# Gated cross-attention and MoE block: the beginning of the kernel rebuilt, keys made batch by batch

## The chip, the cores and the metric

One core of one Trainium2 chip. The figure is device time in microseconds (us) of one execution; it is measured over three runs and the median is compared. TensorE (PE), VectorE (DVE), ScalarE (ACT), GpSimd (POOL) and SyncE (SP, which here only issues DMAs) each run their own instructions in program order and wait for each other by semaphores.

## What is computed

Four batches of 256 positions of width 256 pass through gated cross-attention to a context of width 64 (16 query heads, 4 key heads, head width 16), and then through a second gated block: causal attention with 16 heads of width 128, and a mixture of four experts.

```python
x = x + tanh(g_xattn[0]) * xattn(layernorm(x), ctx, ctx, q_norm_w, k_norm_w, w_out)
x = x + tanh(g_ffn[0]) * ffn(layernorm(x), ...)      # attention 16x128, then MoE, top 2 of 4

def xattn(q, k, v, q_norm_w, k_norm_w, w_out):
    q, k = rms_norm(q, q_norm_w), rms_norm(k, k_norm_w)
    q, k = q * cos + rotate_half(q) * sin, k * cos + rotate_half(k) * sin   # per head of 16
    scores = einsum('bgnqd,bgkd->bgnqk', q, k) / sqrt(16)                   # causal mask, softmax
    return (softmax(scores) @ v).reshape(B, T, 256) @ w_out.T
```

## The kernel before

Everything stays in SBUF; a position is a partition, so a batch b is two tiles t of 128 positions. The change touches only what leads into cross-attention and the first part of it.

**The packed operands.** Scores are made by bf16 products that keep float32 accuracy: a query or key head of 16 numbers is split in three bf16 parts (value, rest, rest of the rest), and the parts are repeated in eight *slots* of 16, which fill the 128 rows of a product. Queries of a batch are made in two halves X of 8 heads. `qpack` (written as q_room) and `kpack` (written as V) hold these slots, and PE turns them (eight transpositions each: `q_turn(b, X, t)` L1161, `k_turn(b)` L1150) into PSUM banks 6 and 7, from where ACT (`q_evac` L527) copies them to qT (qk_room) and DVE (`k_out` L802) to kT (yacc). Each of the two banks serves a fixed order of users (the lists M6 and M7), and each user waits until the one ahead has been copied out.

**The beginning.** DVE takes the statistics of batch 0 (`stats(0, 2)`, L743 and L746), then, once ACT has summed the squares of all eight context tiles (L517), runs three Newton steps for ten reciprocal roots (L723 to L725), normalizes the queries of batch 0 (`norm_q(0)`, L763), and makes the keys of all four batches at once (L768 to L787) with the tables WKC and WKS that POOL makes first (L329 to L331). POOL goes on with the query tables WC and WS (L338 to L340) and `prep(b, X)` (L353 to L366), which rotates one half of the queries and writes three of the eight slots. `pack(b, X)` on DVE (L793 to L797) fills the other five.

**The pieces.** Scores then go in 48 pieces p, twelve to a batch (k is the piece in its batch b). In a piece PE runs `x_scores(p)` (L1204, L1205), DVE takes the maxima (`x_max(p)`, L894), PE makes the scores again transposed and shifted by the maxima (`x_turned(p - 3)`, L1218 to L1230), ACT exponentiates them (`x_exp`, L563), and every third piece PE multiplies by the values (`x_values`, L1245) and turns the result (`o_turn`, L1255). `x_scores(p)` waits for the maxima of piece p - 2. Each engine has its own hand-written sequence over p; between the pieces stand the preparations of the next batch: on DVE `norm_q(b + 1)` at k = 1, `pack(b + 1, 0)` at k = 6, `pack(b + 1, 1)` at k = 11, and from batch 1 on the residual and the norm of the batch before; on PE `q_turn(b, 1, t)` at k = 3 and 4, `q_turn(b + 1, 0, t)` at k = 9 and 10, and `out_turn` and `out_project` at k = 8 and 9.

In POOL's order after prep(0, 1) come the copies of the context into the value slots (L392), and then prep(1, 0), prep(1, 1), prep(2, 0) and so on; the split of the first weights of the next stage follows prep(3, 1) (L403 and on).

## Time and profile before

| | us |
|---|---|
| median of 3 runs | 477.19 (476.87 to 477.73) |
| the profiled execution, its own time | 475.73 |
| its span, first to last instruction | 473.9 |
| first maxima of a piece (p = 0) start | 30.12 |
| first maxima of batch 1 (p = 12) start | 47.41 |
| last maxima (p = 47) start | 113.0 |

Busy shares over the whole span: PE 87%, DVE 81%, POOL 60%, ACT 58%. The profile's rows give the start of an instruction or a group from the span's start, its duration, engine, line and tiles; the bracket behind gives the idle time of that engine just before and what ended it. The rows used are shown further down.

### The profile page before, as it was taken

To read this page: it belongs to the slowest core of one execution; us is meant where nothing else is said; L and a number is where in the kernel's file an instruction comes from. 1 tells how busy PE (TensorE), PEld (TensorE's weight loads), DVE (VectorE), ACT (ScalarE), POOL (GpSimd) and SP (SyncE) were. 2 spreads that over 40 slices of the span, in tenths; PEclk is the share of its full clock that TensorE was granted. 3 is DMA by queue.
4 is the path that set the end of the run, shared out by engine and by line. 5 is a ranking of instruction groups with operands and counts; after the bars stand their busy time and mean duration, and the time that the engine had idled before them with its cause. 6 is when DMAs were issued, how large, how long until landed. Compare 5 with 4: busy or idle time off the path is not lost.

```text
span 473.9 us, 10279 instructions
## 1 busy us (share of the span) xinstructions
PE 413.9 (87%) x3150; PEld 360.1 (76%) x3150; DVE 383.0 (81%) x1185; ACT 273.6 (58%) x617; POOL 286.0 (60%) x385
## 2 busy tenths in 40 slices
PE   0179998889899699999999999999999996678994
PEld 0157876667677599899899899898998995567894
DVE  4886769695889688798797897898898768867997
ACT  2036655554235567766767687677677688175440
POOL 5956718902299557777587586687687544153541
PEclk9999999999999799999999999999999998799998
DMA  8200000200245496585775765775865754000011
GB/s 279 57 3 1 2 1 3 89 2 1 46 100 123 85 190 134 127 201 109 160 169 117 181 145 109 190 138 117 194 134 111 145 89 92 20 0 2 0 46 44
DMA packets 71347, 44.53 MB, mean 94 GB/s; under 512 B 57360, under 2 KB 59536, under 8 KB 71312
## 3 DMA queue, kind: packets, MB, share of 16 engines
q1 hardware_dynamic: 67392, 35.42, 35.2%
q10 hardware_dynamic: 3920, 8.69, 6.6%
q8 instruction: 17, 0.28, 0.2%
q14 instruction: 18, 0.15, 0.1%
HBM read 13.68 MB, written 1.05 MB: 31 GB/s over the span
## 4 chain that ended last, share of the span: by engine, by line
PE 64%; DVE 21%; POOL 6%; issue 5%; ACT 2%; DMA 2%; ACTq 0%; SPq 0%; DVEq 0%; POOLq 0%
PE bank L1264 35%; PE bank L1332 5%; PE bank L1378 5%; DVE yacc L1119 3%; PE bank L1331 3%; PE bank L1379 3%; DVE yacc L1128 2%; DVE nxm L894 2%; PE bank L1245 2%; PE bank L1204 2%; PE bank L1182 2%; DMA rows_sb<-in_rows 1%; POOL room L435 1%; PE bank L1161 1%; PE bank L1205 1%
## 5 line engine op out<-in xcount | busy, mean ns | idle before, releaser
L630 ACT ACTIVATE probs<-sm,nm 128x128 f32<-128x128 f32 (+1 forms) x128 | 56.9, 447 | 43.3 <-DVE nm L1005 43.3
L622 ACT ACTIVATE probs<-turned 128x768 uint16<-128x768 uint16 x64 | 69.1, 1079 | 20.9 <-DMA turned<-halves 20.0
L1264 PE MATMUL bank<-hH,qk_parts 128*128 128x512 f32 x240 | 75.6, 396 | 0.0
L447 POOL COPY halves<-probs 128x768 uint16<-128x768 uint16 x64 | 52.8, 825 | 37.3 <-DVE probs L1051 36.5
L435 POOL TENSOR_TENSOR room<-room,qk_room 128x512 f32<-128x512 f32 x32 | 41.3, 1293 | 34.6 <-DMA qk_room<-qk_room 29.5
L1264 PE MATMUL bank<-hL,qk_parts 128*128 128x512 f32 x120 | 58.3, 486 | 0.5 <-DVE room L922 0.4
L1264 PEld LDWEIGHTS bank<-hH,qk_parts 128*128 128x128 f32 x240 | 45.5, 190 | 9.6
L922 DVE SCALAR_TENSOR_TENSOR room<-bank,qk_bias,cst_sb 128x512 f32<-128x512 f32 x64 | 47.4, 740 | 0.0
L1264 PE MATMUL bank<-woH,o_parts 128*128 128x256 f32 x256 | 47.3, 283 | 0.0
L1264 PE MATMUL bank<-woL,o_parts 128*128 128x256 f32 x128 | 38.8, 303 | 6.5 <-DVE yacc L1042 2.5
L435 POOL TENSOR_TENSOR room<-room,q_room 128x512 f32<-128x512 f32 x32 | 41.2, 1290 | 5.4 <-DMA q_room<-q_room 5.4
L1264 PE MATMUL bank<-wvL,hH 128*128 128x256 f32 x128 | 39.3, 307 | 5.0 <-POOL wvL L380 4.3
L639 ACT ACTIVATE o_parts<-bank,bv_pair 128x256 fp32r<-128x256 f32 x64 | 30.0, 468 | 19.1 <-PE bank L1379 12.7
L563 ACT ACTIVATE probs<-bank 128x512 f32<-128x512 f32 x48 | 28.5, 596 | 21.5 <-PE bank L1230 12.6
L894 DVE TENSOR_REDUCE nxm<-bank 128x2 bf16<-128x512 f32 (+1 forms) x48 | 32.4, 686 | 10.0 <-PE bank L1205 9.6
L1264 PEld LDWEIGHTS bank<-woH,o_parts 128*128 128x128 f32 x256 | 39.6, 190 | 0.0
L1378 PE MATMUL bank<-probs,V 128*128 128x256 f32 x128 | 39.3, 390 | 0.0
L1332 PE MATMUL bank<-room 128*128 128x256 f32 x128 | 38.7, 384 | 0.0
L1264 PE MATMUL bank<-wvH,hH 128*128 128x256 f32 x128 | 36.6, 286 | 0.0
L1264 PE MATMUL bank<-wvH,hL 128*128 128x256 f32 x128 | 36.6, 286 | 0.0
L527 ACT ACTIVATE qk_room<-bank 128x1024 bf16<-128x1024 bf16 x16 | 16.4, 1024 | 34.8 <-PE bank L1161 34.8
L922 DVE SCALAR_TENSOR_TENSOR qk_room<-bank,qk_bias,cst_sb 128x512 f32<-128x512 f32 x32 | 24.0, 749 | 15.3 <-PE bank L1264 15.1
(216 smaller groups left out, 1268.8 us busy)
## 6 DMA issues: line engine op xcount, KB each, us to landing
qk_room<-qk_room SPq DMA_DIRECT2D x64, 128.0 KB, 2.4
q_room<-q_room SPq DMA_DIRECT2D x64, 128.0 KB, 2.4
stg<-in_wqkv ACTq DMA_DIRECT2D x6, 768.0 KB, 5.4
stge<-in_we ACTq DMA_DIRECT2D x7, 256.0 KB, 3.0
stg<-in_wqkv SPq DMA_DIRECT2D x2, 768.0 KB, 6.2
stgo<-in_wo ACTq DMA_DIRECT2D x6, 256.0 KB, 3.3
x_sb<-in_x SPq DMA_DIRECT2D x4, 256.0 KB, 6.1
turned<-halves SPq DMA_TRANSPOSE x64, 2.8
```

The source lines that it names most:

```text
L435: pool.tensor_tensor(v, v, qk_sw[q], ALU.subtract).then_inc(s["rope_done"], 1)
L447: pool.tensor_copy(halves[:, j % 2, :, :], PR[:, j % 2, 0:384].bitcast(U16).rearrange("p (n h) -> p h n", h=2)).then_inc(s["b_split"], 1)
L527: act.activation(qT[:, X, t, :, :].rearrange("p h n -> p (h n)"), bank_bf[0][:, :], ACT.Copy).then_inc(s["m6_free"], 1)
L563: act.activation(prob_slot(m, z), PT_B[p % 2][:, :], ACT.Exp).then_inc(s["s_exp"], 1)
L622: act.activation(PTs[:, 1 - q, 0:384].bitcast(U16).rearrange("p (n h) -> p h n", h=2), turned[:, (j - 3) % 4, :, :].rearrange("p (h c) n - ...
L630: ins = act.activation(PR[:, q, a:e], sm[:, q, a:e], ACT.Exp, bias=nm[:, q, t:t + 1], scale=-1.0, accum_out=rs[:, q, t:t + 1])
L639: act.activation(oH[:, ((j - 4) // 2) % 2, q, :], value_bank(j)[:, 0:256], ACT.Identity, bias=head_bias(j)).then_inc(s["b_oH"], 1)
L894: dve.tensor_reduce(nxm[:, m % 3, a:a + len(heads)], S_B[p % 2][:, :].rearrange("p (h n) -> p h n", h=len(heads)), AX.X, ALU.max, negate=T ...
L922: return dve.scalar_tensor_tensor(out.rearrange("p (b t) -> p b t", b=2), source[:, :].rearrange("p (b t) -> p b t", b=2), qk_bias[:, c:c ...
L1264: ins = pe.matmul(outp, l, r, start=(m == 0), stop=(m == n - 1))
L1332: pe.matmul(S_B[j % 2][:, P:3 * P], QT[:, 2 * r, second], QT[:, 2 * r + 1, both], start=True, stop=True).then_inc(s["b_s"], 1)
L1378: pe.matmul(value_bank(j)[:, 0:256], V[:, 2 * b, r * HD:(r + 1) * HD], PTs[:, q, 0:256], start=True, stop=False)
```

## The change

- **Loads.** SP issues x of batch 0, then only the strict mask and the small rope tables, then the identity on a semaphore of its own, and then waits for x of batch 0 and the first rows before it issues the rest. ACT issues the first 320 columns of the rows and the context of batch 0; the other three batches of the context and the rest of the rows it issues after two sums of squares.
- **ACT** makes the bf16 identity and mask (DVE did), sums squares one at a time (each waits for the one ahead, since all write one scratch tile), waits for both late loads ahead of the third, and fills the slots of batch 0's queries and keys (`q_slots`, `k_slots`).
- **DVE** waits for two sums of squares and not eight, and roots four numbers and not ten; it rotates and splits X = 0 of batch 0's queries itself, one tile t at a time. The statistics of batches 1 to 3 move behind the maxima of pieces 1 and 2, their roots (queries and keys, twelve numbers) behind those of pieces 3, 4 and 5, and norm_q(1) from piece 1 to piece 5. `qn` has two buffers. `pack(1, 0)` moves from piece 6 to 8. `k_out(b + 1)` stands behind a piece of batch b.
- **POOL** makes keys, one batch at a time (`keys(b)`): keys(0) after the first query tables, keys(1) between prep(1, 0) and prep(1, 1), keys(2) ahead of prep(2, 0), keys(3) ahead of prep(3, 0). prep(0, 0) is gone (DVE does it).
- **PE** starts with 20 products of 128x512 on the identity that nobody reads. `q_turn(0, 0, 1)` goes to bank 2 and DVE copies it; `q_turn(0, 1, t)` stands at pieces 4 and 5 (3 and 4 before); `k_turn(1)` at piece 10 and `k_turn(b + 1)` at k = 7 of batches 1 and 2. Before, all four key turns stood ahead of piece 0.

```diff
         @block.scalar
-            act.dma_start(ctx_sb[:, :, :], ctx_v).then_inc(s["d_ctx"], 16)
-            act.dma_start(rows_sb[:, :], rows.to_broadcast([P, R_END])).then_inc(s["d_rows"], 16)
+            act.dma_start(rows_sb[:, 0:R_BO], ...).then_inc(s["d_rows"], 16)
+            act.dma_start(ctx_sb[:, 0:2, :], ctx_v[:, 0:2, :]).then_inc(s["d_ctx"], 16)
...
             for t in range(NT):
-                ins = act.activation(kf2[:, t, :], ctx_sb[:, t, :], ACT.Square, accum_out=small[:, 8 + t:9 + t])
+                if t in (0, 2):
+                    act.wait_ge(s["d_ctx"], 16 if t == 0 else 32)
+                if t == 2:
+                    act.wait_ge(s["d_rows"], 32)
+                if t:
+                    act.wait_ge(s["ssk_done"], t)
+                ins = act.activation(squares, ctx_sb[:, t, :], ACT.Square, accum_out=small[:, 8 + t:9 + t])
...
+            q_slots(0, 0)
+            k_slots(0)
             q_evac(0, 0, 0)
-            q_evac(0, 0, 1)
+            k_slots(1)
+            k_slots(2)
+            q_slots(0, 1)
             for p in range(NPX + VLAG):
+                if p == 4:
+                    act.wait_ge(s["q_parts"], 2)
+                    q_slots(1, None)
...
         @block.vector, the pieces
-                if p == 0:
-                    rsqrt_step(SM(124, 6), SM(56, 6), SM(130, 6), 6)
                 if p == 1:
-                    pack(0, 1)
-                if k == 1 and b + 1 < B:
+                    stats(2, 4)
+                if p == 2:
+                    stats(4, NT)
+                if p == 3:
+                    dve.wait_ge(s["ssk_done"], NT)
...
+                if p in (3, 4, 5):
+                    rsqrt_step(SM(70, 12), SM(54, 12), SM(82, 12), 12)
+                if k == (5 if b == 0 else 1) and b + 1 < B:
                     norm_q(b + 1)
+                if k and next_k_at(b, k - 1):
+                    k_out(b + 1)
...
-                if k == 6 and b + 1 < B:
+                if k == (8 if b == 0 else 6) and b + 1 < B:
                     pack(b + 1, 0)
...
         @block.tensor
-            k_turn(0)
+            for _ in range(20):
+                pe.matmul(bank[6][:, :]..., ident_bf, ident_bf.unsqueeze(1).to_broadcast([P, 4, P]), start=True, stop=True)
             q_turn(0, 0, 0)
-            k_turn(1)
+            k_turn(0)
             q_turn(0, 0, 1)
-            k_turn(2)
-            k_turn(3)
             for p in range(NPX + VLAG):
...
+                    if next_k_at(b, k):
+                        k_turn(b + 1)
```

**ACT at the start.** Before, its first instructions (the last row shown is the first copy of turned queries):

```order
L513 DMA ctx_sb<-in_ctx 128x8x64
L514 DMA rows_sb<-in_rows 128x578
L517 ACTIVATE yacc,small<-ctx_sb 128x64 [waits d_ctx]
L517 ACTIVATE yacc,small<-ctx_sb 128x64 x7
L520 ACTIVATE small<-rows_sb 128x2 [waits d_rows]
L527 ACTIVATE qk_room<-bank 128x1024 [waits m6_pe] x3
```

Now, from the first squares (L587) to the first slots (L645 of the changed kernel):

```order
L587 ACTIVATE nh,small<-ctx_sb 128x64 [waits ssk_done]
L591 DMA ctx_sb<-in_ctx 128x6x64 [waits d_rows]
L592 DMA rows_sb<-in_rows 128x258
L587 ACTIVATE nh,small<-ctx_sb 128x64 [waits ssk_done,d_rows,d_ctx]
L587 ACTIVATE nh,small<-ctx_sb 128x64 [waits ssk_done] x5
L593 ACTIVATE small<-rows_sb 128x2
L645 ACTIVATE q_room<-q_room 128x8x32 [waits q0_part] x2
L645 ACTIVATE q_room<-q_room 128x8x16 [waits q0_part]
L652 ACTIVATE V<-V 128x8x16 [waits k0_part]
L654 ACTIVATE V<-V 128x8x16
L600 ACTIVATE qk_room<-bank 128x1024 [waits m6_pe]
```

The wait for two late loads now stands ahead of the first slots.

**DVE in the first pieces.** Before, from the last key copy (L802) on:

```order
L802 COPY yacc<-bank 128x1024 [waits m7_pe,dve_seq]
L894 TENSOR_REDUCE nxm<-bank 128x4 [waits s_pe]
L723 TENSOR_TENSOR small<-small 128x6
L724 TENSOR_TENSOR small<-small 128x6 [waits dve_seq]
L725 SCALAR_TENSOR_TENSOR small<-small 128x6 [waits dve_seq]
L894 TENSOR_REDUCE nxm<-bank 128x2 [waits s_pe,dve_seq]
```

Now (L979 is the maxima, L837 and L840 the statistics):

```order
L979 TENSOR_REDUCE nxm<-bank 128x4 [waits s_pe]
L979 TENSOR_REDUCE nxm<-bank 128x2 [waits s_pe]
L837 BN_STATS bnst<-x_sb 128x6 [waits d_x1]
L837 BN_STATS bnst<-x_sb 128x6
L840 BN_AGGR mv<-bnst 128x2 [waits dve_seq]
L840 BN_AGGR mv<-bnst 128x2
L979 TENSOR_REDUCE nxm<-bank 128x2 [waits s_pe,dve_seq]
L837 BN_STATS bnst<-x_sb 128x6 [waits d_x2]
```

The statistics that stood ahead of piece 0 now stand between its successors.

**POOL in batch 0.** Before, from the end of prep(1, 0) into prep(1, 1):

```order
L365 TENSOR_TENSOR G<-G,q_room 128x256 [waits pool_seq]
L366 CAST q_room<-G 128x16x16 [waits pool_seq]
L353 TENSOR_TENSOR G<-qn,WC 128x256 [waits m6_pe,q_parts]
L355 TENSOR_TENSOR G<-qn,WS 128x8x8
L356 TENSOR_TENSOR G<-qn,WS 128x8x8
```

Now, between the same two, keys(1); its first three products (L399 to L401) stand ahead of these rows, and L376 begins prep(1, 1):

```order
L402 TENSOR_TENSOR k_room<-k_room 128x128 [waits pool_seq]
L404 TENSOR_TENSOR k_room<-k_room,small 128x128 [waits k_scale,pool_seq]
L407 CAST V<-k_room 128x8x16 [waits pool_seq]
L414 TENSOR_TENSOR k_room<-k_room,V 128x128 [waits pool_seq]
L407 CAST V<-k_room 128x8x16 [waits pool_seq]
L414 TENSOR_TENSOR k_room<-k_room,V 128x128 [waits pool_seq]
L407 CAST V<-k_room 128x8x16 [waits pool_seq]
L417 COPY V<-V 128x8x48 [waits pool_seq]
L418 COPY V<-V 128x8x32
L376 TENSOR_TENSOR G<-qn,WC 128x256 [waits m6_pe,kpack_ready]
```

Twelve instructions have come between the two halves of the next batch's queries.

## Rows read from the trace of the kernel before

**Rows 1.** The page: the chain that ended last, share of the span by engine.
```profile
PE 64%; DVE 21%; POOL 6%; issue 5%; ACT 2%; DMA 2%; ACTq 0%; SPq 0%; DVEq 0%; POOLq 0%
```

**Rows 2.** Stretches: length, then PE, PEld, DVE, ACT, POOL busy, clock, DMA.
```profile
47.40:68.70 21.30, 21.30 (x291) 17.38 (x290) 14.03 (x38) 13.30 (x22) 10.31 (x22) 1.00 0.01 2
68.70:95.30 26.60, 22.54 (x308) 17.28 (x305) 22.27 (x57) 14.09 (x24) 21.06 (x40) 1.00 0.13 42
```

**Rows 3.** Timeline of the first loads and their waiters: start, us, engine, what [idle].
```profile
0.73 0.45 SPq L261 DMA_DIRECT2D x_sb<-in_x  x1
...
1.28 0.60 ACTq L514 DMA_DIRECT2D rows_sb<-in_rows  x1
...
4.97 0.26 ACT L517 ACTIVATE yacc<-ctx_sb 128x64 f32<-128x64 f32 x1 [1.78 <-DMA ctx_sb<-in_ctx]
5.14 0.19 ACT L517 ACTIVATION_READ_ACCUMULATOR yacc<-ctx_sb 128x1 f32 x1
...
5.55 0.23 DVE L732 CAST bf_sb<-cst_sb 128x128 bf16<-128x128 f32 x1 [5.55 <-DMA cst_sb<-in_cst]
...
7.03 0.34 POOL L329 TENSOR_TENSOR WKC<-rows_sb,cst_sb 128x64 f32<-128x64 f32 x1 [5.05 <-DMA rows_sb<-in_rows]
```

**Rows 4.** The tile x_sb: its four loads, issue to landing.
```profile
DMA to landing us min/median/max: 3.2/6.1/6.6
```

**Rows 5.** Timeline of DVE: statistics, first and last of the roots, norm_q(0).
```profile
5.82 0.74 DVE L743 BATCH_NORM_STATS2 bnst<-x_sb 128x6 f32<-128x256 f32 x2
...
7.02 0.17 DVE L753 TENSOR_SCALAR small<-small 128x8 f32<-128x8 f32 x1
...
9.93 0.74 DVE L763 TENSOR_SCALAR qn<-x_sb,mv,small 128x256 f32<-128x256 f32 x2
```

**Rows 6.** Timeline: first turn, a copy of turned queries, last key turn, first maxima.
```profile
18.88 1.01 PE L1150 MATMUL bank<-bf_sb,V 128*128 128x128 bf16 x8 [18.88 <-DVE V L787]
...
24.29 1.02 ACT L527 ACTIVATE qk_room<-bank 128x1024 bf16<-128x1024 bf16 x1 [17.10 <-PE bank L1161]
...
28.79 0.62 PE L1150 MATMUL bank<-bf_sb,V 128*128 128x128 bf16 x8 [1.66 <-DVE yacc L802]
...
29.52 0.69 DVE L802 COPY yacc<-bank 128x1024 bf16<-128x1024 bf16 x1 [0.31 <-PE bank L1150]
30.12 0.68 DVE L894 TENSOR_REDUCE nxm<-bank 128x4 bf16<-128x512 f32 x1
```

**Rows 7.** Timeline of POOL: a table product, prep(1, 0), prep(1, 1) to its last row.
```profile
8.46 0.45 POOL L338 TENSOR_TENSOR WC<-rows_sb,cst_sb 128x128 f32<-128x128 f32 x1
...
33.40 0.73 POOL L353 TENSOR_TENSOR G<-qn,WC 128x256 f32<-128x256 f32 x1 [5.22 <-DVE qn L763]
...
37.80 0.67 POOL L365 TENSOR_TENSOR G<-G,q_room 128x256 f32<-128x256 f32 x1
38.54 0.40 POOL L366 CAST q_room<-G 128x256 bf16<-128x256 f32 x1
39.02 0.77 POOL L353 TENSOR_TENSOR G<-qn,WC 128x256 f32<-128x256 f32 x1
...
44.19 0.40 POOL L366 CAST q_room<-G 128x256 bf16<-128x256 f32 x1
```

**Rows 8.** The page: the costliest groups, a copy on POOL (mean ns of one).
```profile
L447 POOL COPY halves<-probs 128x768 uint16<-128x768 uint16 x64 | 52.8, 825 | 37.3 <-DVE probs L1051 36.5
```

**Rows 9.** Timeline of DVE: pack(1, 0) to the next maxima, then pack(1, 1) likewise.
```profile
38.97 0.23 DVE L793 COPY q_room<-q_room 128x256 bf16<-128x256 bf16 x1 [1.21 <-POOL q_room L366]
...
40.63 1.27 DVE L894 TENSOR_REDUCE nxm<-bank 128x2 bf16<-128x512 f32 x2
...
46.73 0.22 DVE L793 COPY q_room<-q_room 128x256 bf16<-128x256 bf16 x1
...
47.41 0.68 DVE L894 TENSOR_REDUCE nxm<-bank 128x4 bf16<-128x512 f32 x1
```

**Rows 10.** Timeline of PE: the first product of the scores of piece 15.
```profile
50.45 0.22 PE L1204 MATMUL bank<-yacc,qk_room 128*128 128x128 bf16 x1
```

More of the change, by code:

```diff
@@ L186, in prob_slot @@
             return probs[:, 3 * (m % 2) + z, :]
-        M6, M7 = [("Q", 0, 0, 0), ("Q", 0, 0, 1)], [("K", b) for b in range(B)]
+        M6, M7 = [("Q", 0, 0, 0)], [("K", 0), ("K", 1), ("K", 2)]
         for b in range(B):
@@ L196, in build_kernel, with k_scale, second_q_at, next_k_at @@
         NPX = XP * B
+        def k_scale(b):
+            return 34 if b == 0 else 58 + 2 * b
+        def second_q_at(b, k):
+            return k - (4 if b == 0 else 3)
+        def next_k_at(b, k):
+            return b + 1 < B and k == (10 if b == 0 else 7)
         def steps(eng, step, peeled=1):
@@ L331, in _, with q_tables @@
                 pool.tensor_tensor(wks[:, :, 8:16], w[:, :, 0:8], sn[:, :, 8:16], ALU.mult).then_inc(s["wtab_ready"], 1)
-            for X in range(2):
+            def q_tables(X):
                 for t in range(2):
@@ L367, in prep, with keys @@
                 pool.wait_ge(s["q_parts"], 2 * b + X + 1)
+            def keys(b):
+                both = lambda room: room.rearrange("p (t n) -> p t n", t=2)
+                kv = ctx_sb[:, 2 * b:2 * b + 2, :]
+                heads = lambda room: room.rearrange("p (n d) -> p n d", d=XD)
+                sines = WKS[:, :, :].rearrange("p t (g d) -> p (t g) d", d=XD)
+                kc = kv.rearrange("p t (g d) -> p (t g) d", d=XD)
+                pool.tensor_tensor(both(kf), kv, WKC[:, :, :], ALU.mult)
+                pool.tensor_tensor(heads(kf2)[:, :, 0:8], kc[:, :, 8:16], sines[:, :, 0:8], ALU.mult)
+                link(pool.tensor_tensor(heads(kf2)[:, :, 8:16], kc[:, :, 0:8], sines[:, :, 8:16], ALU.mult))
+                link(pool.tensor_tensor(kf, kf, kf2, ALU.add))
+                pool.wait_ge(s["k_scale"], 1 if b == 0 else 2)
+                link(pool.tensor_tensor(both(kr), both(kf), small[:, k_scale(b):k_scale(b) + 2].unsqueeze(2).to_broadcast([P, 2, 64]), ALU.mult))
+                part = kpack[:, 8 * b:8 * (b + 1), :, :]
+                for m in range(3):
+                    ins = pool.tensor_copy(part[:, :, m, :], heads(kr))
+                    if b == 0:
+                        ins.then_inc(s["k0_part"], 1)
+                        pool.wait_ge(s["k0_part"], m + 1)
+                    else:
+                        link(ins)
+                    if m < 2:
+                        link(pool.tensor_tensor(heads(kr), heads(kr), part[:, :, m, :], ALU.subtract))
+                if b == 0:
+                    return
+                pool.tensor_copy(part[:, :, 3:6, :], part[:, :, 0:3, :])
+                pool.tensor_copy(part[:, :, 6:8, :], part[:, :, 0:2, :]).then_inc(s["kpack_ready"], 1)
+                pool.wait_ge(s["kpack_ready"], b)
+            q_tables(0)
+            pool.wait_ge(s["wtab_ready"], 6)
+            pool.wait_ge(s["d_ctx"], 16)
+            keys(0)
+            q_tables(1)
             def low_qk(c, p):
@@ L789, in pack @@
+            dve.memset(small[:, 110:111], 0.0).then_inc(s["q_parts"], 1)
             def pack(b, X):
```

188 lines of the change are left out of this document (114 added, 74 removed).

## The prediction, made before the changed kernel was run

> **What bounds the kernel now.** I read the chain of waits first, then the busy time by stretches, then the timeline of the first 50 us engine by engine. Over the whole span PE leads the chain with 64% [rows 1]; POOL has 6%, most of it at the start, in the table products and prep(0, 0). Nothing behind the maxima of the last piece is touched, so the question is by how much the pieces end sooner. Their first maxima start at 30.12 [rows 6], and from there three regimes follow. In batch 0 the pieces wait for their feeding: POOL takes up norm_q(1) at 33.40 and has both halves of the next queries at 44.59 [rows 7]; the maxima of piece 12 come at 47.41 [rows 9]. In batch 1 PE is busy for 21.30 of 21.30 us [rows 2]: a time won at its entry is kept. In batch 2 PE (22.54 of 26.60) and DVE (22.27) take turns [rows 2]. I therefore follow the change to one point, the scores of piece 15, which PE starts at 50.45 [rows 10], and treat what lies behind as moved by the same amount, apart from what the change adds there.
>
> **Loads and first sums.** DVE's first work waited until 5.55 for the constants, its statistics began at 5.82, and POOL's tables waited for the rows until 7.03 [rows 3, 5]. x of batch 0 was issued at 0.73 and the quickest of the x loads took 3.2 [rows 3, 4], so it was there at 3.9. With 640 KB in front instead of 1,025 KB I put the first loads at 4.0 to 4.6 (bounds 3.9 and 7.03). ACT then makes identity and mask (0.6, two casts of about the 0.26 of row L517 or a little more) and two sums of 0.43 each (0.26 + 0.19 less overlap [rows 3]): 6.1. Roots took 7.02 to 9.93 = 2.9 [rows 5]; most of that is a fixed cost per instruction, so four numbers instead of ten save nothing: 9.0, against 9.93. The two query halves on DVE (norm 0.4, then ten small operations at 0.2 to 0.4, with POOL beside them) cost some 3.2 each: 12.2 and 15.4. POOL's tables, keys(0) and prep(0, 1) end at about 12.9 and 21.8. None of these is latest.
>
> **What is latest: ACT.** Ahead of the first slots ACT waits for the two loads that it issued itself behind its second sum, the last one at 6.6. Landing: 3.2 later is 9.8, the quickest load seen [rows 4]; 5.7 later is 12.3, what the rows took before (1.28 to 7.0 [rows 3]), with 545 KB on ACT's queue against 324 now. I take **10.4**, nearer the short end since the queue is shorter. Then, in ACT's order: six sums one at a time 2.6 (before they overlapped; the wait on the one ahead forbids it now), tanh 0.2, q_slots(0, 0) 1.0, k_slots(0) 0.55, the copy of the first turn 1.1 (1.02 [rows 6] and a hand-over), k_slots(1) and (2) 0.8, q_slots(0, 1) 1.0; then PE's turn 0.7 (0.62 to 1.01 [rows 6]) and DVE's copy of it 0.7 (0.69, L802 [rows 6]). The slot copies have no row of their shape; 64 columns took 0.26 and 1,024 took 1.02 [rows 3, 6], between which 128 to 256 columns give 0.25 to 0.4. Together 8.65: **the first maxima start at 19.1**, 11 us before 30.12.
>
> **Why that is not the gain.** Work that stood ahead of piece 0 now stands between pieces 0 and 5 on DVE, and norm_q(1) stands behind it: six maxima at 0.6 (0.68 less overlap [rows 6]) 3.6, statistics of two tiles 1.1 and of four 2.0 (5.82 to 7.02 for two with their first small operation [rows 5]), roots 2.9, norm_q 0.75 [rows 5]: 10.35. POOL gets norm_q(1) at **29.5**, against 33.40: of 11 us, 3.9 are left. Should ACT's slots for X = 1 (q_parts at 21.8, then 1.5, two turns and two copies of 1.02) be later, they hold the scores of piece 6 at about 28, which is no later than DVE.
>
> Then POOL: prep(1, 0) 5.62 (33.40 to 39.02 [rows 7]); keys(1), which is new here: five products of 128x128 and 128x64 at 0.28 to 0.5 (0.45 [rows 7]) 2.1, three casts and two differences 2.0 (half the width of 0.40 and 0.67 [rows 7], plus the wait on each), two copies of 384 and 256 columns 1.0 (between 0.40 for 256 and 0.825 for 768 [rows 7, 8]): **5.1**, bounds 4.3 and 6; prep(1, 1) 5.57 (39.02 to 44.59 [rows 7]). Together 16.3: **45.8**, against 44.59. pack(1, 1), behind which the maxima of piece 12 are queued, took 0.68 with POOL idle and 1.66 with POOL at work (46.73 to 47.41 and 38.97 to 40.63 [rows 9]); POOL now goes straight on with keys(2), so I take 1.6. Then maxima 12 (0.6), the norm of an output (0.45) and maxima 13 (0.7): the scores of piece 15 at **49.2**, against 50.45: 1.25 sooner. PE, which had finished everything else by then, has no work of its own later than that.
>
> The trace shows DVE's copies at 1.66 beside POOL and 0.68 without it. The Trainium skill (SBUF — State Buffer, Who interferes with whom) says that copies of this kind on VectorE and GpSimd's instructions exclude each other for a whole instruction; by that rule pack(1, 1) is the long one, and with the short one the scores of piece 15 would come 0.95 sooner. It speaks against moving the keys to POOL, and the trace agrees as far as pack goes.
>
> **What is added behind.** Two key turns and their copies leave the beginning and enter batches 1 and 2: 0.45 each on PE (0.62 less the last product's tail of about 0.2 [rows 6]), the copies of 0.69 on DVE. In batch 1 PE has no gap, so 0.45 counts; in batch 2 PE has 4 us of gaps [rows 2] and I count half, 0.2. keys(2) and keys(3) end at about 51 and 66, where POOL was idle. In sum 1.25 - 0.65 = **0.6 us** sooner. The 20 idle products, some 3 to 8 us on an idle PE from 5.4, cost nothing unless they last beyond 13. The profiled execution had 475.73 with a span of 473.9, the median of the runs is 477.19; taken from the median, 0.6 less is **476.6**.
>
> **Rivals.**
> - *The late loads don't hold ACT.* If they land before 9 and ACT's small copies are as short as DVE's, the two halves on DVE (15.4) come last: first maxima at 16.8, norm_q(1) at 27.2, scores of piece 15 at 46.9, 3.5 sooner, less 0.65: **474.3**. For it: the quickest load took 3.2 [rows 4]. Against: x2 and x3 took over 6 on a full queue [rows 4], and SP issues 1.5 MB just ahead.
> - *Slower: the late loads land late.* Each microsecond of landing passes to norm_q(1), to POOL and to piece 15 undiminished. The break-even is a landing at 11.0 (norm_q(1) at 30.1); at 12.3, the upper bound, the scores of piece 15 come at 51.1, 0.65 later, and with 0.65 added behind: **478.5**. keys(b) at 6 instead of 5.1 does the same with 0.9 us.
> - *PE slows down while it waits for keys.* Eight turns took 1.01 at 18.88 and 0.62 at 28.79 [rows 6], a distance of 0.11 and 0.057 between turns: the paces of 1.2 and 2.4 GHz, though the column of the granted clock reads 1.00 over the whole stretch. In the changed kernel PE stands from about 35 to 40.2, until keys(1) is there. If it then runs at the slow pace, the key turn, a query turn, piece 7's second scores and values and the scores of piece 11, some 2.7 us at the 1.78 per piece of batch 1 [rows 2], take 5.4; the maxima of 11 and the key copy end at 47.0 instead of 44.4, and pack(1, 1), otherwise ready at 45.8, starts 1.2 later. **477.8**, or 478.8 with what PE then has to catch up. The Trainium skill (TensorE: Matmul & The Clock Gate, HAM oscillation — how this bites in real kernels) describes this: waits between bursts of products bring the half rate back each time. No stretch of before shows it past the first maxima, since there PE never stands that long.
> - *The start passes through.* If POOL's chain were not what piece 12 waits for, up to 11 us would stay, 466. Against it: POOL's 16.3 in a row behind norm_q(1), all by rows.
>
> **Chances.** The forecast, POOL's chain giving most of it back, 50%, with a range of its own of 475.2 to 477.8 (keys 4.3 to 6, landing 9.8 to 11.2). Loads that don't hold 20%, passing through 2%, late landing 15%, slow PE 13%. A difference under 0.2% (0.95 us) can't be told from none here. Of the forecast's 50%, 22 lie below 476.2, 25 within, 3 above 478.1; early loads and passing through are faster; late landing is slower in 14 of 15; slow PE is slower in 8 and within in 5. Faster 0.44, same 0.31, slower 0.25. For the range I leave out one in ten at each side: 473.8 to 478.8.
>
> **What the profile after would show.** First maxima between 18 and 20.5, and ahead of the first slots a wait of ACT for a DMA of context or rows that ends near 10.4. norm_q(1) taken up by POOL at 29.5; DVE without long gaps between pieces 0 and 5. POOL without a gap from there to 45.8, and DVE waiting for it ahead of both packs and PE ahead of k_turn(1). The scores of piece 15 at 49.2. Wrong would be: a gap on POOL between prep(1, 0) and prep(1, 1) (then PE or DVE sets the pace); keys(1) far from 5.1; turns at 0.11 behind 40; or a first piece as late as 22.

## The result: 0.9% slower, and the profile after

The changed kernel took 481.66 us (median of 7 runs, 479.76 to 484.07), the kernel before 477.19 beside it (7 runs, 475.34 to 478.79): a ratio of 1.0094, 95% interval 1.0071 to 1.0117. The forecast was 476.6, its range ended at 478.8. The profiled execution took 480.99 with a span of 478.8, against 475.73 and 473.9.

The first maxima did come 6.5 us sooner, and all of it was gone by piece 12. The chain of waits of the changed kernel up to 60 us, cut (start, us, what), tells it in order:

```profile
1.77 3.92 DMA cst_sb<-in_cst
5.72 0.31 ACT bf_sb L577
6.94 7.73 DMA rows_sb<-in_rows
14.74 0.36 ACT nh L587 x2
...
17.95 1.05 PE bank L1265 x8
...
23.64 1.33 DVE nxm L979 x2
...
32.94 0.42 DVE qn L858
33.44 0.72 POOL G L376
...
39.02 0.49 POOL k_room L399
...
44.14 0.72 POOL G L376
```

7.73 us of this chain are one transfer: the second part of the rows, which ScalarE issued at 6.94 and for which it waits ahead of its third sum of squares. ACT's rows, where [rows 3] stood before, have the wait in the bracket:

```profile
6.50 0.40 ACTq L591 DMA_DIRECT2D ctx_sb<-in_ctx  x1
6.94 0.57 ACTq L592 DMA_DIRECT2D rows_sb<-in_rows  x1
14.74 0.26 ACT L587 ACTIVATE nh<-ctx_sb 128x64 f32<-128x64 f32 x1 [7.90 <-DMA rows_sb<-in_rows]
```

POOL's rows, which answer to [rows 7], show norm_q(1) taken up at the old time (33.40 before), the keys in between, and the second preparation done at 49.67 instead of 44.59:

```profile
33.44 0.72 POOL L376 TENSOR_TENSOR G<-qn,WC 128x256 f32<-128x256 f32 x1 [9.17 <-DVE qn L858]
...
38.55 0.40 POOL L389 CAST q_room<-G 128x256 bf16<-128x256 f32 x1
39.02 0.49 POOL L399 TENSOR_TENSOR k_room<-ctx_sb,WKC 128x128 f32<-128x128 f32 x1
...
43.66 0.40 POOL L418 COPY V<-V 128x256 bf16<-128x256 bf16 x1
44.14 0.72 POOL L376 TENSOR_TENSOR G<-qn,WC 128x256 f32<-128x256 f32 x1
...
49.27 0.40 POOL L389 CAST q_room<-G 128x256 bf16<-128x256 f32 x1
```

DVE's, which answer to [rows 9], show it waiting for that ahead of both packs. The maxima of piece 12 start at 50.94, 3.53 us later than before:

```profile
38.98 0.23 DVE L886 COPY q_room<-q_room 128x256 bf16<-128x256 bf16 x1 [2.43 <-POOL q_room L389]
...
47.00 0.69 DVE L979 TENSOR_REDUCE nxm<-bank 128x2 bf16<-128x512 f32 x1 [2.72 <-PE bank L1311]
47.61 0.68 DVE L895 COPY yacc<-bank 128x1024 bf16<-128x1024 bf16 x1
49.70 0.23 DVE L886 COPY q_room<-q_room 128x256 bf16<-128x256 bf16 x1 [1.41 <-POOL q_room L389]
...
50.94 0.68 DVE L979 TENSOR_REDUCE nxm<-bank 128x4 bf16<-128x512 f32 x1
```

The stretches that answer to [rows 2] (length, then PE, PEld, DVE, ACT and POOL busy, clock, DMA): batch 1 (first row) is half a microsecond longer, and PE has gaps in it now. The last three numbers are the granted clock, the DMA share and GB/s.

```profile
50.94:72.75 21.81, 20.67 (x280) 16.49 (x274) 14.87 (x39) 12.54 (x21) 18.18 (x43) 1.00 0.01 2
72.75:99.48 26.73, 22.75 (x310) 17.71 (x312) 22.16 (x58) 14.08 (x24) 21.04 (x40) 1.00 0.12 42
```

PE's records of batch 1 are 280 where there were 291, and a few can be missing, so its busy time is a little too low; its rows show three pauses of 0.16 to 0.54 us there. So the span's 4.9 us are: 3.53 by piece 12, 0.63 from there to the last maxima (117.20 against 113.04), and 0.7 behind them. That last part of the kernel is untouched; over the profiles of this page it took 360.9 to 363.8 us whatever was changed, so 0.7 is within what it varies by itself.

### The profile page after: what moved, and what is told of

Read it like the earlier page. It is cut to its first block, busy times and chain, and to the rows that moved or that the text cites. A ratio compares the mean times of both kernels' runs of the same rounds, so it can differ in the third digit from the quotient of the medians.

```text
span 478.8 us, 10369 instructions
## 1 busy us (share of the span) xinstructions
PE 422.7 (88%) x3155; PEld 364.8 (76%) x3170; DVE 378.5 (79%) x1185; ACT 278.0 (58%) x632; POOL 294.1 (61%) x420
## 4 chain that ended last, share of the span: by engine, by line
PE 61%; DVE 20%; POOL 6%; issue 5%; DMA 3%; ACT 3%; SPq 0%; ACTq 0%; POOLq 0%; DVEq 0%
PE bank L1370 35%; PE bank L1439 5%; PE bank L1485 5%; DVE yacc L1215 3%; PE bank L1438 3%; DVE nxm L979 2%; PE bank L1486 2%; DVE yacc L1224 2%; DMA rows_sb<-in_rows 2%; PE bank L1286 2%; PE bank L1351 1%; POOL room L495 1%; PE bank L1310 1%; PE bank L1265 1%; DVE small L824 1%
## 5 line engine op out<-in xcount | busy, mean ns | idle before, releaser
L1370 PE MATMUL bank<-woH,o_parts 128*128 128x256 f32 x256 | 48.9, 289 | 0.0
L1370 PEld LDWEIGHTS bank<-woH,o_parts 128*128 128x128 f32 x256 | 41.0, 197 | 0.0
L979 DVE TENSOR_REDUCE nxm<-bank 128x2 bf16<-128x512 f32 (+1 forms) x48 | 32.6, 687 | 10.4 <-PE bank L1311 9.7
L561 POOL TENSOR_TENSOR qk_parts<-G,o_parts 128x512 fp32r<-128x512 f32 x16 | 21.7, 1370 | 23.4 <-ACT o_parts L797 23.1
```

The source lines that it names most:

```text
L561: pool.tensor_tensor(GL[:, (n // 2) % 2, n % 2, :], G[:, n % 2, :], GH[:, (n // 2) % 2, n % 2, :].bitcast(F32), ALU.subtract).then_inc(s[" ...
L979: dve.tensor_reduce(nxm[:, m % 3, a:a + len(heads)], S_B[p % 2][:, :].rearrange("p (h n) -> p h n", h=len(heads)), AX.X, ALU.max, negate=T ...
L1370: ins = pe.matmul(outp, l, r, start=(m == 0), stop=(m == n - 1))
```

## The experiments

Theory 1, in the numbers of the texts below: both late loads hold ACT, ACT holds the first piece, DVE's work between the pieces passes that on to norm_q(1), and POOL's 16.3 us behind it set the entry to batch 1. The others, with some rivals that have no number, are told in the expectations: theories 1a and 2a are two causes of the slow landing, 3 and 4 the idle products (the 20 that nobody reads), 5 the hand-overs between the engines at pieces 5 to 11, 6 the slow pace of TensorE. The numbering skips 9. Each kernel is the changed one with the edit shown. The marks of each profile, in us, and the ratio to the kernel before, run beside it:

| kernel | ACT's third sum | first maxima | norm_q(1) on POOL | maxima of 12 | last maxima | median, ratio (95%) |
|---|---|---|---|---|---|---|
| before | | 30.12 | 33.40 | 47.41 | 113.04 | |
| after | 14.74 | 23.64 | 33.44 | 50.94 | 117.20 | 481.66, 1.0094 (1.0071 to 1.0117) |
| e1 squares late | 17.6 | 19.83 | 29.64 | 47.20 | 114.96 | 477.47, 0.9993 (0.9962 to 1.0023) |
| e2 stats gap | 15.14 | 26.33 | 24.62 | 47.12 | 113.78 | 478.27, 1.0023 (0.9997 to 1.0050) |
| e3 loads first | 7.55 | 20.33 | 30.31 | 48.34 | 114.60 | 478.36, 1.0024 (0.9999 to 1.0048) |
| e4 keys short | 13.18 | 21.67 | 31.46 | 48.55 | 115.24 | 478.61, 1.0031 (1.0003 to 1.0058) |
| e5 no idle | 15.54 | 24.51 | 34.26 | 52.16 | 119.83 | 480.43, 1.0081 (1.0054 to 1.0109) |
| e6 SP hold | 11.11 | 19.85 | 29.66 | 47.17 | 113.41 | 477.57, 1.0019 (0.9992 to 1.0046) |
| e7 both | 8.15 | 27.45 | 25.74 | 48.70 | 115.76 | 478.54, 1.0031 (1.0004 to 1.0058) |
| e8 batch 1 roots | 17.7 | 19.63 | 26.02 | 48.96 | 115.64 | 479.63, 1.0056 (1.0032 to 1.0079) |
| e10 hold, roots | 11.79 | 19.88 | 26.98 | 44.62 | 110.96 | 475.25, 0.9964 (0.9938 to 0.9990) |
| e11 hold, roots, warm | 10.91 | 18.98 | 26.60 | 44.18 | 111.86 | 476.24, 0.9985 (0.9964 to 1.0007) |
| e12 hold, warm | 11.50 | 19.18 | 29.02 | 46.54 | 112.79 | 477.75, 1.0011 (0.9981 to 1.0041) |
| e13 keys ahead | 11.70 | 19.97 | 27.32 | 43.33 | 110.91 | 473.77, 0.9926 (0.9900 to 0.9951) |

### Is it the wait of ACT? Squares late, and loads first

```diff
-            for t in range(NT):     # six sums, behind the wait for both late loads
+            for t in range(2):
 ...
             q_slots(0, 1)
+            for t in range(2, NT):
+                square(t)
+            act.activation(small[:, 96:98], rows_sb[:, R_GX:R_GX + 2], ACT.Tanh)...
```

> The changed kernel with one edit: ScalarE's sums of squares of tiles 2 to 7, with their wait for the two late loads, and the tanh stand behind its slots for batch 0 and not ahead of them. Theory 1 (the two late loads, landed at 14.7 us, hold ScalarE and through its slots the first piece, DVE's roots and norm_q(1)): ScalarE's first slots start near 14.3 when DVE's first query part is there instead of at 17.0, the second tile's near 17.5; the first maxima move from 23.64 to about 20.7, POOL takes up norm_q(1) at about 30.6 instead of 33.44, and the whole kernel is about 2.8 us shorter, 478.9 against 481.66. Rival (something else, such as TensorE's slow pace or DVE's work, sets the first pieces): first maxima may move but norm_q(1) stays within 0.5 us of 33.4 and the time within 1 us of 481.7.

Loads first keeps the order of the sums and issues both late loads at once, each with a semaphore of its own:

```diff
             act.dma_start(ctx_sb[:, 0:2, :], ctx_v[:, 0:2, :]).then_inc(s["d_ctx"], 16)
+            act.dma_start(ctx_sb[:, 2:NT, :], ...).then_inc(s["d_ctx2"], 16)
+            act.dma_start(rows_sb[:, R_BO:R_END], ...).then_inc(s["d_rows2"], 16)
```

> The changed kernel with one edit: ScalarE issues the context of batches 1 to 3 and the rest of the rows at once behind its first two loads, on semaphores of their own, and not behind its second sum of squares. Theory 1 (issued at 6.5 to 7.5 behind SyncE's list of large loads they took 7 to 8 us; issued first they land before 8): ScalarE no longer stands from 6.9 to 14.7, the first maxima come near 20.5 to 21, norm_q(1) near 30.5, time about 479, as in the run with the squares moved; the first constants and x land 0.5 to 1 us later than in the changed kernel. Rival (the 256-byte pieces of the context are slow whenever they are issued): the wait ends beyond 11 and the gain is under 1.5 us.

In both the first maxima come 3.3 to 3.8 us sooner, norm_q(1) 3.1 to 3.8, piece 12 2.6 to 3.7, and both kernels are back at the time of before. The wait of ACT passes on as far as piece 12, nearly whole. Squares late has no wait for the late loads ahead of its slots at all, and yet its first maxima come at 19.83 and no sooner: without the loads it is DVE's two query halves, done at 14.2 and 17.4, that the first slots and turns wait for.

### Is it POOL behind it? Statistics in the gap, and keys left out

Statistics and roots of batches 1 to 3 and norm_q(1) move ahead of the first key copy, where DVE waited:

```diff
+            stats(2, NT)
+            ...                     # roots of twelve numbers
+            norm_q(1)
             k_out(0)
             dve.wait_ge(s["q_first_pe"], 1)
```

> The changed kernel with one edit: DVE makes the statistics and roots of batches 1 to 3 and norm_q(1) right behind its own query halves, ahead of the first key copy, and not between the first six pieces. Theory 1 (the chain norm_q(1), prep(1,0), keys(1), prep(1,1) on POOL, 16.3 us in a row, sets the entry to batch 1, so what counts is when norm_q(1) is done): norm_q(1) is done near 24 instead of 33.4, POOL has both halves of the next queries near 41 instead of 49.7, although the first maxima come later, near 26. The entry to batch 1 then is bound by TensorE's own work on twelve pieces, some 17 to 18 us behind the first maxima, near 44 instead of 50.9: 6 to 7 us shorter, about 475. Rival (the first maxima are what counts, or POOL's keys cost DVE and TensorE elsewhere): the kernel gets slower by the 2 to 3 us by which the first maxima move back, 484.

Keys short leaves out the rotation, scaling and splitting of the keys of batches 1 to 3 and writes one raw copy of the context instead, so its output isn't the reference's:

```diff
             def keys(b):
+                if b:
+                    pool.tensor_copy(kpack[:, 8 * b:8 * (b + 1), :, :], raw...)
+                    return
```

> The changed kernel with part of the computation left out: the keys of batches 1 to 3 are not rotated, scaled and split; POOL only copies the raw context into their slots, one copy instead of twelve instructions each. Theory 1 (keys(1), measured at 5.1 us between the two preparations, lies fully on the path to batch 1): that stretch shrinks to about 1.2, POOL's last part of batch 1 comes at 45.8 instead of 49.7, and the time falls by 3.5 to 4 us, to about 478. Rival (another wait ends at the same time, such as TensorE's turns or DVE's maxima): under 1.5 us.

Here theory 1 fell short. POOL had norm_q(1) at 24.62 in the one and 3.9 us less to do in the other, but from norm_q(1) to piece 12 took 22.5 and 17.1 us, against 17.5 in the changed kernel: of 8.8 us and of 3.9 us only 3.8 and 0.4 arrived. With the statistics in the gap POOL had both halves done at 40.87, 16.25 us behind norm_q(1), but the pieces began at 26.33 and needed 20.8 us to piece 12. DVE waited for PE ahead of piece 11 and not for POOL ahead of pack(1, 1), and the granted clock was 1.00 from 32 to 48:

```profile
45.08 0.69 DVE L989 TENSOR_REDUCE nxm<-bank 128x2 bf16<-128x512 f32 x1 [1.87 <-PE bank L1308]
45.69 0.68 DVE L895 COPY yacc<-bank 128x1024 bf16<-128x1024 bf16 x1
46.29 0.22 DVE L886 COPY q_room<-q_room 128x256 bf16<-128x256 bf16 x1
```

In keys short DVE's rows show a pack(1, 0) that lasts 2.2 us beside POOL, a piece 11 that waits for PE, and no wait for POOL at all ahead of pack(1, 1):

```profile
37.17 1.06 DVE L892 COPY q_room<-q_room 128x256 bf16<-128x256 bf16 x1
...
46.52 0.69 DVE L984 TENSOR_REDUCE nxm<-bank 128x2 bf16<-128x512 f32 x1 [3.02 <-PE bank L1316]
47.12 0.68 DVE L900 COPY yacc<-bank 128x1024 bf16<-128x1024 bf16 x1
47.72 0.22 DVE L891 COPY q_room<-q_room 128x256 bf16<-128x256 bf16 x1
```

and its stretches (columns as above) that PE had half its clock there:

```profile
36.00:40.00 4.00, 0.62 (x7) 0.63 (x8) 2.89 (x6) 0.00 (x0) 3.79 (x8) 0.75 0.00 0
40.00:44.00 4.00, 3.78 (x29) 3.26 (x29) 1.19 (x3) 1.62 (x2) 3.51 (x8) 0.50 0.00 0
```

So POOL is the longest chain of the changed kernel only by the 1.41 us that DVE waits for it; next comes pack(1, 0), two turns and pieces 9 to 11 at the slow pace. How much the keys are worth in time is less sure than the marks look: the median of keys short is 3 us under that of the changed kernel, with some 1.7 us either way, while its profile's last maxima come 2.0 sooner, 1.6 of which is its earlier landing (13.18).

### Why 7.7 us for a load? SyncE held back, and the idle products

```diff
             sp.dma_start(x_sb[:, 6:8, :], ...)
+            sp.wait_ge(s["d_ctx"], 32)
+            sp.wait_ge(s["d_rows"], 32)
             sp.dma_start(cols_sb[:, :], cols).then_inc(s["d_cols"], 16)
```

> One edit: SyncE issues its columns, mask, rope tables and weights only when both late loads of ScalarE have landed (x of batches 1 to 3 still go out ahead). It tells why the late loads, issued at 6.5 and 6.9, took 6.9 and 7.7 us. Theory 1a (they stand behind what SyncE has put on the same 16 DMA engines, 1.5 MB): landing near 10.5 (bounds 10 to 12) instead of 14.7, first maxima near 19.5 to 20.5, norm_q(1) on POOL at 29.5 to 30.5, maxima of piece 12 at 47 to 48, time 477.5 to 479 as in the two kernels that took the wait from ahead of the slots. Theory 2a (many small packets of their own: six tiles of 256-byte lines and a row repeated to 128 partitions, slow on ScalarE's queue whoever else is on): landing stays at 13.5 or later, time 481 or more. If the weights land later than they are used, the maxima of piece 12 come early but the stretch behind the last maxima grows instead.

> The changed kernel without the 20 products that nobody reads; all else as changed. They ran from 6.28 to 12.1 us, TensorE then stood 5.8 us, and its first turns were at the slow pace all the same (1.03 us for eight, granted clock 0.50 at 16 to 24 us). Theory 1 (late landing of the two late loads and POOL's chain of 16.3 us set the entry to batch 1): no change, first maxima within 0.5 of where the landing puts them, maxima of piece 12 within 0.5 of 50.9, time 481 to 482. Theory 3 (the products keep SBUF or TensorE's queue from the start, or their end delays the turns): first turn and first maxima over 0.5 us sooner, time 480 or less. Theory 4 (they do warm the clock for what comes later): turns and first pieces slower, pieces 0 to 5 take over 1 us more, time 482.5 or more.

With SyncE's other transfers held back, the same two loads, issued at the same time, were there 3.6 us sooner. ACT's row in this kernel:

```profile
11.11 0.26 ACT L589 ACTIVATE nh<-ctx_sb 128x64 f32<-128x64 f32 x1 [4.30 <-DMA rows_sb<-in_rows]
```

The tile of the rows, its two loads, in the changed kernel (the last number is the second part):

```profile
DMA to landing us min/median/max: 3.7/5.7/7.7
```

and the same view here:

```profile
DMA to landing us min/median/max: 3.7/3.9/4.2
```

Every mark follows, and down to piece 24 they are within 0.1 us those of squares late. The cause of the slow landing is thus shown: it is what SyncE put on the queue in the meantime (cols, mask, rope, 768 KB of wqkv and three times 256 KB, issued from 6.46 on), and not the small pieces of the loads themselves. The Trainium skill (DMA: Bandwidth & Descriptors, Issuing engines are not separate DMA queues) says that transfers of different issuers run on the same 16 engines and interleave; 7.7 against 4.2 us agrees.

Those transfers come with and behind the two loads. The 768 KB of x that SyncE issues just ahead of them, at 5.0, are not held back in this kernel, and the loads took 4.2 us behind them all the same. The landing also varies by itself: the second part of the rows took 6.3 to 8.5 us in the six kernels that issue it as the changed one does, and 4.1 to 4.8 in the five that hold SyncE back.

The kernel without the idle products, whose edit is to drop the loop of 20, is as slow as the changed one, and its own landing, 15.54, moved its marks by 0.8 to 1.2 us. No effect of the products shows.

Squares late and no idle have their last maxima 1.4 us later than their piece 36 lets expect: that last batch took 19.2 us, against 17.7 in every other kernel. Their stretches show a dip of PE's clock that the others don't have, after the pause with which the batch begins (squares late):

```profile
95.00:100.00 5.00, 2.93 (x31) 2.53 (x27) 4.62 (x20) 0.98 (x2) 0.00 (x0) 0.82 0.01 2
100.00:105.00 5.00, 4.78 (x61) 3.84 (x61) 3.52 (x12) 3.52 (x6) 0.00 (x0) 0.84 0.02 3
```

The same pause at 95 to 100 in SP hold (PE busy 2.92 of 5) went by at 1.00. No edit touches that place, so I take it that a profile's last maxima can be 1.4 us off by chance, and compare pieces 12 to 24 first.

### Both at once, and roots for one batch only

Both (loads first and statistics in the gap) and the roots of batch 1 only, with squares late:

```diff
-                if p == 1:
-                    stats(2, 4)
+                if p == 0:
+                    stats(2, 4)
+                    ...             # seed and step for the 4 numbers of batch 1
+                if p == 1:
+                    ...             # two steps
+                    norm_q(1)
+                if p == 6:
+                    stats(4, NT)
+                ...                 # roots of 8 numbers behind pieces 7 to 10
```

> Both late loads issued at once behind the first two, and statistics and roots of batches 1 to 3 in DVE's gap ahead of the first key copy. Theory 1 (POOL's chain behind norm_q(1)): norm_q(1) at about 24 on POOL, its 16.3 us end at 40.7; the first piece, no longer held by a landing, at 22.5 to 23.5 (18.5 when the halves are done, 5 us of statistics and roots on DVE), and from there TensorE's own pace, 1.78 us a piece as in batch 1: maxima of piece 12 at 43.5 to 45, last maxima 3 us sooner than in the kernel with the statistics in the gap alone (110.5 to 112), time 474.5 to 476. Theory 5 (what gave the loss back in four different kernels is one common wait behind POOL, the hand-overs of TensorE, ScalarE and DVE at pieces 5 to 11, some 47 us whatever is moved): maxima of piece 12 at 46.5 or later, time 477.5 to 478.5.

> The six late sums of squares behind the first slots (as in the first experiment), and of the statistics and roots only those of batch 1 ahead of norm_q(1), behind the maxima of pieces 0 and 1; those of batches 2 and 3 behind the maxima of pieces 6 to 10, where DVE waited for POOL. Theory 1: first maxima at 19.8 as there; norm_q(1) on POOL at 19.8 + two maxima 1.3 + statistics of two tiles 1.1 + seed and three steps 2.4 + norm 0.75 = 25.4 instead of 29.6; POOL's chain ends at 41.6, pack 1.2: maxima of piece 12 at 43 to 44 instead of 47.2, last maxima at 111 to 112, time 473.5 to 475.5. Theory 5 (hand-overs at pieces 5 to 11 come to the same 47): maxima of piece 12 at 46 or later, time 477 to 478.

Both missed what theory 1 gave, and piece 12 came where theory 5 had put it. POOL had norm_q(1) 7.4 to 7.7 us sooner than in the changed kernel, and piece 12 came 2.0 to 2.2 us sooner. In the first, POOL was done at 41.99, but the first maxima came only at 27.45 (22.5 to 23.5 expected), the pieces needed 21.3 us from there, and pack(1, 1) started at 47.87 without a wait for POOL. In the second, PE stood 2.90 us while DVE rooted, and its next turns were at the slow pace; then pack(1, 0), for which POOL was done at 31.54, waited until 38.83 behind pieces 6 to 8 and the statistics and roots of the later batches on DVE, and PE 3.65 for it. PE's rows:

```profile
24.17 0.22 PE L1324 MATMUL bank<-yacc,qk_room 128*128 128x128 bf16 x1 [2.90 <-DVE nxm L984]
...
27.83 1.03 PE L1279 MATMUL bank<-bf_sb,q_room 128*128 128x128 bf16 x8 [0.36 <-ACT q_room L647]
...
40.74 0.62 PE L1279 MATMUL bank<-bf_sb,q_room 128*128 128x128 bf16 x8 [3.65 <-DVE q_room L895]
```

### The same, placed so that nobody stands

SyncE held back; statistics of batch 1 behind piece 1, its roots behind 2 and 3, norm_q(1) behind 3; statistics and roots of batches 2 and 3 behind pieces 8 (after pack(1, 0)), 9 and 10:

```diff
+                if p == 2:
+                    ...             # seed and first step, 4 numbers
+                if p == 3:
+                    ...             # two steps
+                if k == (3 if b == 0 else 1) and b + 1 < B:
                     norm_q(b + 1)
 ...
                     pack(b + 1, 0)
+                if p == 8:
+                    stats(4, NT)
+                ...                 # roots of 8 numbers behind pieces 9 and 10
```

> SyncE holds back as in the sixth experiment, and the statistics and roots of batch 1 alone stand ahead of norm_q(1), spread behind the maxima of pieces 1, 2 and 3; those of batches 2 and 3 behind pieces 8, 9 and 10, after pack(1, 0). Different from the eighth experiment, no gap of 3 us opens on TensorE ahead of piece 2, and nothing of the later batches stands ahead of pack(1, 0). Theory 1 (norm_q(1) plus POOL's 16.3 us is the entry to batch 1): first maxima 19.9, norm_q(1) on POOL at 26.5 instead of 29.7, pack(1, 0) near 32.2, maxima of piece 12 at 44.0 to 44.8 instead of 47.17, last maxima 110.2 to 111, time 474.5 to 475.8. Theory 5 (the pieces' own hand-overs between TensorE, ScalarE and DVE are only a little behind POOL): norm_q(1) at 26.5, but maxima of piece 12 at 46 or later, time 476.5 to 477.5.

This one did what theory 1 says, mark by mark: 26.98 against 26.5 expected, piece 12 at 44.62 against 44.0 to 44.8, the last maxima at 110.96 against 110.2 to 111, and 475.25 us, 0.36% under the kernel before. DVE's rows and PE's clock show why it could: pack(1, 0) starts on time, ahead of the later statistics, and PE's clock reads 1.00 from 24 to 48 us (0.57 at 36 to 40 in SP hold).

```profile
32.59 0.22 DVE L888 COPY q_room<-q_room 128x256 bf16<-128x256 bf16 x1
...
43.39 0.23 DVE L888 COPY q_room<-q_room 128x256 bf16<-128x256 bf16 x1 [1.11 <-POOL q_room L391]
...
44.62 0.68 DVE L981 TENSOR_REDUCE nxm<-bank 128x4 bf16<-128x512 f32 x1
```

The stretches of the same kernel, PE first and the clock third from the end:

```profile
36.00:40.00 4.00, 2.25 (x45) 1.90 (x45) 3.69 (x15) 1.26 (x3) 3.71 (x10) 1.00 0.02 4
40.00:44.00 4.00, 2.76 (x37) 2.10 (x30) 2.78 (x9) 1.56 (x4) 3.57 (x8) 1.00 0.01 2
```

### Longer idle products, and keys begun early

```diff
-            for _ in range(20):
+            idle(28)                # into a bank of scores
             q_turn(0, 0, 0)
+            idle(7)
```

> The sixth experiment (SyncE holds back until the late loads are there) with the same stretched idle products, 28 and 7. It prices the slow pace by itself. Theory 6: key turn and second query turn 0.62 instead of 1.03 to 1.04 each, first scores at half the time: first maxima at 19.0 instead of 19.85; DVE has no gap from there to norm_q(1), so norm_q(1) at 28.8 to 29.0 instead of 29.66, and the maxima of piece 12 at 46.4 instead of 47.17: 476.8 to 477. If the products make no difference to the pace, all marks stay within 0.2 us; if they come too late and hold the first turn back, the first maxima come later than 19.85.

> As the tenth, with the idle products stretched to bridge the pauses: 28 instead of 20 ahead of the first turn (0.2 us each by then, so until some 13.9 us) and 7 more behind it. Theory 6 (TensorE stands at the slow pace between 16 and 24 us because it stood still before, and that costs time): the turns of 16.9 and 17.8 take 0.62 instead of 1.03, the granted clock of 16 to 20 us is over 0.9 instead of 0.50, first maxima at 19.0, last maxima 0.5 to 1 us sooner than in the tenth. Theory 1 alone (DVE and POOL set pieces 0 to 5): turns as fast, but norm_q(1) at most 0.8 sooner and last maxima within 0.8 of the tenth.

With the pauses bridged the three first turns took 0.62 each and the first maxima came at 19.18 and 18.98, 0.7 and 0.9 us sooner. Piece 12 still had 0.6 and 0.4 of it. The times show nothing of it (1.0011 and 0.9985, with intervals that overlap those without). In the second, by its stretches, PE's clock fell later, after a stretch in which PE was busy for 1.81 of 4 us, and the lead was lost there:

```profile
40.00:44.00 4.00, 1.81 (x17) 1.12 (x16) 3.62 (x12) 0.78 (x2) 3.60 (x8) 0.92 0.01 2
44.00:48.00 4.00, 4.00 (x45) 2.88 (x44) 2.76 (x8) 1.45 (x3) 3.43 (x10) 0.66 0.00 0
```

Last, e10 with the first part of keys(1) in POOL's gap ahead of norm_q(1):

```diff
+            keys(1, 0)              # the products that need no root
             prep(1, 0)
-            keys(1)
+            keys(1, 1)
```

> As the tenth, with one edit on GpSimd: the first four products of keys(1), which need neither the roots nor norm_q(1), stand behind the context copies, where GpSimd stood idle from 24.3 to 26.98, and no longer between prep(1, 0) and prep(1, 1). They took 1.69 us there (32.59 to 34.28). Theory 1 (GpSimd's work behind norm_q(1) sets the entry to batch 1, a microsecond of it is a microsecond of time): norm_q(1) still taken up at 27.0, prep(1, 1) starts at 36.1 instead of 37.77 and ends at 41.7, maxima of piece 12 at 43.0 (bounds 42.8 and 43.6) instead of 44.62, last maxima at 109.3 to 110, time 1 to 1.7 us under the tenth against the kernel before, a ratio of 0.993 to 0.9955. Theory 5 (TensorE and VectorE are next, just behind): VectorE had only 1.1 us of waiting left ahead of pack(1, 1) in the tenth, so the maxima of piece 12 stop at 43.6 or later and at most 1.0 us is won; ratio 0.9955 to 0.997.

Piece 12 came at 43.33, inside the bounds, but the last maxima at 110.91, where e10 has them: PE was busy for 1.76 us between 40 and 44, its clock was 0.72 there and 0.86 in the next 4 us, and piece 15 came at 48.13 against 47.52. So of the 1.3 us at piece 12 this profile shows none at the end. The time, the median of six executions, is 473.77 us or 0.74% under the kernel before, the lowest of all; whether it differs from e10 is open, since the intervals overlap and the marks end alike. Both are faster than either kernel of this case.

## Why the prediction was wrong, point by point

- **Loads and first sums: 0.4 to 2.1 us too early.** x of batch 0 at 5.02 (4.0 to 4.6 put), roots done at 10.36 (9.0), the halves at 14.2 and 17.5 (12.2 and 15.4). None was latest, as said, but the halves come next: squares late has its first maxima at 19.83, where the rival "the late loads don't hold ACT" put 16.8. So with the landing that I took, 10.4, the first maxima would have come near 19.8, and near 19.1 only with all first turns at the fast pace (19.18 and 18.98 in e12 and e11).
- **The late loads: the step that failed.** I took 10.4 with bounds of 9.8 and 12.3; they were there at 14.7. The upper bound was the 5.7 us that the rows took before, issued at 1.28, when SyncE had issued 480 KB; now they were issued in the middle of SyncE's list. I had put "SP issues 1.5 MB just ahead" under what speaks against early loads and let it raise nothing. (The late loads are 321 KB, not 324.) By the trace 0.8 MB stood ahead; 520 and 768 KB followed within 1.1 us, and three times 256 KB behind those. With SyncE held back (11.1) the marks are 19.85, 29.66 and 47.17, and the time is 477.57, 1.0019 of the kernel before. The forecast gives 477.3 for that landing. That is in part luck, for two errors cancel: norm_q(1) and pack(1, 1) together came 0.9 us sooner than summed, and the point of counting (below) was 1.2 too kind.
- **From landing to norm_q(1): right.** 8.9 us to the first maxima (8.65 summed), 9.8 from there to norm_q(1) (10.35). The error of the landing arrived undiminished, since in the changed kernel ACT's wait stays the latest: 29.5 + 4.3 + 0.25 - 0.55 = 33.5, and 33.44 was measured. That is the rival "the late loads land late", of which I wrote just this and which I gave 15% and a worst case of 12.3.
- **POOL's chain: right to 0.1 us.** 5.58, 5.12 for keys(1) (5.1), 5.53: 16.23 against 16.3. pack(1, 1) took 1.24, not 1.6. The Trainium skill (SBUF — State Buffer, Who interferes with whom) has such copies and GpSimd exclude each other; every pack of the first 62 us that ran beside POOL, in all profiles, was long (1.0 to 2.2 us against 0.68 with POOL idle), as with that rule. But that POOL alone sets piece 12 was right only by 1.41 us. In the kernel before it was not POOL at all: it was done at 44.59, and pack(1, 1) came 2.1 us later, behind a piece 11 that waited for PE:

```profile
46.13 0.69 DVE L894 TENSOR_REDUCE nxm<-bank 128x2 bf16<-128x512 f32 x1 [1.57 <-PE bank L1205]
```

- **The point from which I counted: 1.2 us too kind.** The scores of piece 15 started at 52.80, 3.6 later than forecast and 2.35 later than before, but the last maxima are 4.16 later. By piece 12 my own terms give 45.8 + 1.6 = 47.4, the very time of before, and so 0.65 slower; by piece 15 they gave 0.6 faster. From the maxima of 12 to the scores of 15 it took 1.86 us (3.04 before [rows 9, 10]), but from 12 to 24 21.81 (21.30 [rows 2]). I read it so, and no run tests it: behind a pause PE has nothing left over from the pieces before, runs through the next three, and has their second half still ahead. It isn't a time kept. This error alone would have turned the sign of the forecast, inside its range.
- **Added behind: right in size.** 0.65 was put from the key turns; 0.63 was measured between piece 12 and the last maxima. No run leaves the turns out, so that they are its cause is not shown.
- **The slow PE: it came, and cost nothing here.** The turn at 40.34 took 1.03 after 3.53 us of waiting, and the granted clock of 40 to 44 us was 0.60. But DVE still waited 1.41 for POOL afterwards. Where POOL was faster, the clock was low in the stretch in which the lead was lost (0.50 in keys short, 0.66 in e11, 0.72 and 0.86 in e13); with the statistics in the gap a lead was lost at 1.00 too. The Trainium skill (TensorE: Matmul & The Clock Gate, HAM oscillation — how this bites in real kernels) describes such a return to half rate after waits between bursts; these rows agree, but not all do: without idle products the same turn took 0.62 after a wait of 4.03 us.
- **The idle products: nothing, as said.** They ended at 12.1, inside the 13 us allowed, and the kernel without them is no faster.

With the true landing (+4.3) the forecast would have been 480.9, and counted from piece 12, which adds 1.25, a little over 482; 481.66 was measured. So the landing is most of the miss (SP hold gives back 3.8 us at piece 12) and the point of counting the rest.

## What to carry to other kernels

When an engine waits for a load that it issues itself, time the load by what the other issuers put on the DMA engines in those microseconds; order loads by need across all issuers, and put nothing that the load doesn't serve behind its wait. A gain at a first event survives only as far as the next in-order queue whose work was moved behind it, so count from the last point where everyone waits for one event, and not from a point inside the burst that follows. Between pieces, spread the moved work so that no engine waits long and the urgent item stands ahead of the rest: DVE's same instructions gave 1.0056 in one order (e8) and 0.9964 in another (e10). The two kernels also differ in how ACT is freed of the late loads (squares late, SP hold), but these two ways alone gave the same marks down to piece 24.
